# Second block's exponentials: rounded and full both from ScalarE, the low part from GpSimd

## The reference

```python
q = _conv1x1_bn(xf, q_w, ...)          # 16 channels
k = _conv1x1_bn(xf, k_w, ...)
v = _conv1x1_bn(xf, v_w, ...)          # 128 channels
attn = jax.nn.softmax(jnp.einsum('bci,bcj->bij', q, k), axis=-1)
out = jnp.einsum('bcj,bij->bci', v, attn).reshape(b_, c_, h_, w_)
return gamma[0] * out + x
```

## Time and profile before

| | us |
|---|---|
| median of 3 runs | 405.02 |
| lowest and highest of the 3 | 403.21 and 407.89 |
| span of the profiled execution | 403.1 |
| TensorE busy (matmuls) | 341.7 |
| VectorE busy | 260.5 |
| ScalarE busy | 198.8 |
| GpSimd busy | 27.3 |

### The profile page before, as it was taken

One profiled execution on the slowest core, in us unless ns is written; L12 is line 12 of the kernel. 1 busy time (PEld: TensorE's weight loads), 2 busy tenths in 40 slices (PEclk: granted clock), 3 DMA queues, 4 the chain that ended last, 5 costly groups with the idle time before them and its releaser, 6 DMA issues. The chain is left out here.

```text
span 403.1 us, 4422 instructions
## 1 busy us (share of the span) xinstructions
PE 341.7 (85%) x1408; PEld 237.8 (59%) x1408; DVE 260.5 (65%) x425; ACT 198.8 (49%) x351; POOL 27.3 (7%) x35
## 2 busy tenths in 40 slices
PE   3999777999998989999999899996599657597296
PEld 2853644785666847656775686672468356565162
DVE  1576777897598669876977797569397431301605
ACT  2445585646686646385685555667452433211000
POOL 3211100000021000002010000061001000100000
PEclk9999899999999699999998999996697957777579
DMA  7500000000000000000000000059600000000005
GB/s 247 188 0 2 0 1 0 2 0 0 2 0 3 0 0 2 0 0 2 0 0 0 0 0 0 0 192 411 230 2 0 0 2 0 0 0 2 1 0 208
DMA packets 5778, 15.08 MB, mean 37 GB/s; under 512 B 1294, under 2 KB 1998, under 8 KB 5762
## 3 DMA queue, kind: packets, MB, share of 16 engines
q0 software_dynamic: 2304, 8.39, 5.9%
q1 hardware_dynamic: 3458, 6.49, 4.6%
HBM read 12.78 MB, written 2.10 MB: 37 GB/s over the span
## 5 line engine op out<-in xcount | busy, mean ns | idle before, releaser
L373 PE MATMUL acc<-e,v0n 128*128 128x512 f32 x128 | 58.9, 595 | 0.9 <-DVE v0n L828 0.8
L659 ACT ACTIVATE e<-tile,nmax 128x1024 f32<-128x1024 f32 x22 | 24.5, 1115 | 38.8 <-DVE nmax L821 29.1
L860 DVE TENSOR_TENSOR e1l<-e,e1h 128x1024 fp32r<-128x1024 f32 x32 | 39.5, 1248 | 0.7
L373 PEld LDWEIGHTS acc<-e,v0n 128*128 128x128 f32 x128 | 23.5, 189 | 24.6 <-issue 20.1
L698 ACT ACTIVATE e<-tile 128x1024 f32<-128x1024 f32 x25 | 25.7, 1027 | 20.7 <-DVE e1l L860 13.9
L821 DVE TENSOR_REDUCE nmax<-tile 128x1 f32<-128x1024 f32 x22 | 26.9, 1222 | 11.0 <-PE tile L373 10.5
L864 DVE TENSOR_REDUCE nmax<-tile 128x1 f32<-128x1024 f32 x27 | 32.1, 1216 | 2.4 <-PE tile L373 2.4
L373 PE MATMUL tile<-ks,qs 96*128 96x512 f32 (+2 forms) x82 | 27.2, 426 | 6.1 <-ACT tile L688 4.2
L688 ACT ACTIVATE tile<-tile,nmax 128x1024 f32<-128x1024 f32 x27 | 29.4, 1087 | 3.0 <-DVE nmax L864 2.8
L857 DVE CAST e1h<-e 128x1024 fp32r<-128x1024 f32 x32 | 21.7, 687 | 3.5 <-ACT e L698 3.4
L373 PEld LDWEIGHTS tile<-ks,qs 96*128 96x128 f32 x82 | 15.3, 209 | 14.6 <-issue 8.1
(11 more groups left out here) (202 smaller groups left out, 678.6 us busy)
## 6 DMA issues: line engine op xcount, KB each, us to landing
cas_h<-in_cas_h_in POOLq DMA_DIRECT2D x8, 512.0 KB, 9.6
cas_l<-in_cas_l_in POOLq DMA_DIRECT2D x8, 512.0 KB, 10.4
xin<-in_x SPq DMA_DIRECT2D x4, 512.0 KB, 4.7
out<-xin SPq DMA_DIRECT2D x3, 512.0 KB, 2.6
zexp<-in_region_in SPq DMA_DIRECT2D x2, 360.0 KB, 4.7
out<-xin SPq DMA_DIRECT2D x2, 256.0 KB, 2.4
bins<-in_bins_in SPq DMA_DIRECT2D x1, 372.0 KB, 5.1
x3s<-in_near_in SPq DMA_DIRECT2D x1, 288.0 KB, 5.6
```

The source lines that it names most:

```text
L373: return nc.tensor.matmul(o, lhsT, rhs, start=start, stop=stop, skip_group_check=skip)
L659: nc.scalar.activation(e0[:, i % RING0, :], t[:, :], ACT.Exp, bias=nmax0[:, i:i + 1], accum_out=sum0[:, i:i + 1]).then_inc(s["e0_ready"], 1)
L860: vec.tensor_tensor(e1l[:, i % RING, :], e1[:, i % STAGE, :], e1h[:, i % RING, :].bitcast(F32), ALU.subtract).then_inc(s["e1l_ready"], 1)
```

## The change

The round `e1h` and the full `e1` are both written by ScalarE: it reads the score tile twice and takes the exponential twice, first with the short format as its output, then as float32. The wait on `e1_used` that stood ahead of VectorE's cast now stands ahead of ScalarE's first exponential. The subtraction moves from VectorE to GpSimd, which waits for `e1_ready` (and `e1_used`). The steps `e1h:*` leave the lists; TensorE's own order and all places in PSUM are as before.

```diff
@@ STEADY (the same is done in L12_ALL)
-    ... norm0:3 scoreT:0 scoreT:1 e1h:0 gram:4 scoreT:2 e1l:0 e1h:1 e1l:1 mix:2 scoreT:3 gram:5 e1h:2 attend:0 ...
+    ... norm0:3 scoreT:0 scoreT:1 gram:4 scoreT:2 e1l:0 e1l:1 mix:2 scoreT:3 gram:5 attend:0 ...
@@ ScalarE
                     elif name == "scoreT":
                         t = take(step)
 
+                        wait_past(act, s["e1_used"], b * CH + max(i - RING + 1, 0))
+                        nc.scalar.activation(e1h[:, i % RING, :], t[:, :], ACT.Exp).then_inc(s["e1h_ready"], 1)
                         wait_past(act, s["e1l_ready"], b * CH + max(i - STAGE + 1, 0))
                         nc.scalar.activation(e1[:, i % STAGE, :], t[:, :], ACT.Exp).then_inc(s["e1_ready"], 1)
@@ VectorE
-                    elif name == "e1h":
-                        dve.wait_ge(s["e1_ready"], b * CH + i + 1)
-
-                        wait_past(dve, s["e1_used"], b * CH + max(i - RING + 1, 0))
-                        vec.tensor_copy(e1h[:, i % RING, :], e1[:, i % STAGE, :]).then_inc(s["e1h_ready"], 1)
-                    elif name == "e1l":
-                        dve.wait_ge(s["e1h_ready"], b * CH + i + 1)
-                        vec.tensor_tensor(e1l[:, i % RING, :], e1[:, i % STAGE, :],
-                                          e1h[:, i % RING, :].bitcast(F32), ALU.subtract).then_inc(s["e1l_ready"], 1)
@@ GpSimd
+                    elif name == "e1l":
+                        pool.wait_ge(s["e1_ready"], b * CH + i + 1)
+                        wait_past(pool, s["e1_used"], b * CH + max(i - RING + 1, 0))
+                        gp.tensor_tensor(e1l[:, i % RING, :], e1[:, i % STAGE, :], e1h[:, i % RING, :].bitcast(F32),
+                                         ALU.subtract).then_inc(s["e1l_ready"], 1)
```

More of the change, by code:

```diff
@@ L79 @@
     "qkproj:0 qkproj:1 qklow:0 join elu:0 qklow:1 elu:1 zelu:0 zelu:1 score:0 score:1 score:2 score:3 "
[4 rows of a table removed]
-    "xkeep chanT")
[4 rows of a table added]
 END = steps(
```

## The result

The changed kernel takes 415.95 us (median of 4, 414.96 to 416.26), beside 405.51 for the kernel before (median of 4, 403.21 to 407.89): ratio 1.0248, 95% interval 1.0202 to 1.0295. It is slower by 10.4 us.

What follows compares the result with a forecast made beforehand. TensorE was taken as the bound, with no gap in the attend stretches of images 0 to 2. 9.0 there plus 2.2 in the last image, 11.2 us, on 405.0 gave 416; range 411 to 422.

Steps and rivals of the forecast that it cites:

- Part 1: VectorE losing its casts and subtractions: worth 0 in images 0 to 2, some 0.3 us at most in the last.
- Part 2: Second exponential on ScalarE in the attend stretches: its queue order delays TensorE by 2.3 to 2.4 us per image.
- Part 3: Subtraction on GpSimd at 2.40 us each: TensorE waits 0.6 us at the third product of `attend:7`, images 0 to 2.
- Images 0 to 2: Attend stretches of the first three images: 2.4 + 0.6 = 3.0 us each, 9.0 together (2.5 to 3.8 each).
- Part 4: Last image's attend stretch: `attend:0` 1.7 us late, `attend:4` ending 2.1 late by GpSimd; 2.2 taken, bounds 1.4 and 3.0.
- the low clock behind `xproj` follows as before: Last image, behind `attend:4`: `xproj` and its low clock unchanged, giving GpSimd time to finish by 314.2, needed at about 315.
- up to 0.7 was forecast: Last image: `x3:0` and `x3:1` on VectorE meet GpSimd's first subtraction, one waiting for the other, costing up to 0.7 us.
- the last one: Sum over the span: the last image's 2.2 us counted in full, added to the 9.0 for 11.2.
- Hidden: Rival: second exponential and subtraction hide in the attend stretches, so not slower, 404 to 406 us; chance 7%.
- chunk 3: Deciding point of the hidden rival: its rounded exponential must end by the start of `attend:1`, with `gram:5`'s right behind.
- A lower clock in the stretches of images 0 to 2: Rival: gaps around `scoreT:4` lower TensorE's clock once per image, 7.8 us more, 424; chance 10%.
- GpSimd at 2.8: Rival: GpSimd's subtraction takes 2.8 us and bounds the stretches, 4.5 to 4.7 per image, 4 in the last, 422; chance 8%.

Runs made afterwards that it cites:

- e1: The changed kernel with the subtraction back on VectorE, ScalarE still taking both exponentials: 413.5 us, ratio 1.023 to the kernel before.
- e5: The changed kernel with VectorE subtracting and four places for the rounded exponentials: 409.8 us, ratio 1.0105 to the kernel before.
- e4: The kernel before with a useless second exponential of each chunk on ScalarE, cast and subtraction left on VectorE: ratio 1.0099 by two executions (406.7 and 409.4 us).
- e3: The changed kernel with four places for the rounded exponentials instead of three: 410.5 us, ratio 1.0138 to the kernel before.
- e6: The kernel before with the change in the last image alone: 405.9 us, ratio 1.0005 to the kernel before.
- e7: The kernel before with the change in images 0 to 2 alone: 415.8 us, ratio 1.0235 to the kernel before.
- e2: The kernel before with only the subtraction moved to GpSimd, one exponential and VectorE's cast kept: 423.8 us by two executions; ratio 1.0552 takes in all four.
- e8: As e2, but VectorE rounds by a maximum over an axis of length one instead of a cast: 415.9 us, ratio 1.026 to the kernel before.

## Why the prediction was right

It said 416, by order in ScalarE's queue first and GpSimd second, and 415.95 was measured. The two causes are right and were shown in images 0 to 2. That the number agrees within a tenth is luck: the rise was forecast as 11.2 and is 10.4, on a kernel before whose median was taken as 405.0 and is 405.5 with one more run, and several misses below cancel. Point by point, by its own parts:

**Part 1, VectorE relieved: worth nothing.** Right. VectorE idles 12.7 us ahead of `gram:6`'s maximum now, and in images 0 to 2 there was no TensorE gap to close. In the last image the wait of 0.15 for VectorE's `e1l` is gone and one of 0.30 for ScalarE has come ahead of `scoreT:7`. VectorE lost 56 us of busy time, not 61, with 2 us of `x3:1` waiting for GpSimd in there; ScalarE gained 28, not 33, and GpSimd 76 as forecast.

**Part 2, the second exponential.** A rounded exponential takes 1.03 and starts 0.92 apart, as taken. 2.3 to 2.4 were forecast, e1 has 2.6. The gaps stand where they were put; by the starts above, `scoreT:2` lost 0.44 (forecast 0.3), `gram:5` 0.07 (0.2), `attend:0` 0.36 (0.35), `scoreT:4` 1.00 (0.75) and `scoreT:5` 0.62 (0.7). Of the two mechanisms in it, the second reading of a tile costs 1.0 to 1.2 (e5, e4), the wait for `attend` at the head of ScalarE's queue 1.4 to 1.6 (e1 less e4, e1 less e5), or 1.15 when GpSimd subtracts (the changed kernel less e3).

**Part 3, GpSimd.** The duration was taken as 2.40, and is 2.38 to 2.40 in the stretches of images 0 to 2. Forecast 0.6, measured 0.65 (the changed kernel's stretches less e1's), of which 0.43 stands at `attend:7`.

**Images 0 to 2.** 9.0 forecast, 9.8 measured: a term that was sized 0.27 per image too low, for the two pieces above.

**Part 4, the last image: right in sum by luck, largely wrong in how.** 2.2 forecast, 2.4 measured in the stretch. TensorE there, and a window of the clock:

```profile
302.88 0.70 PE L371 MATMUL tile<-qs,ks 96*128 96x512 f32 x2 [1.59 <-DVE v1l L850]
305.21 1.19 PE L371 MATMUL acc<-e1h,v1h 128*128 128x512 f32 x2 [1.63 <-ACT e L698]
...
303.80:307.80 4.00, 2.59 (x6) 2.14 (x7) 2.41 (x1) 3.10 (x4) 4.00 (x2) 0.50 0.00 0
...
310.46 0.64 PE L371 MATMUL acc<-e1h,v1l 128*128 128x512 f32 x2
...
317.54 3.75 PE L371 MATMUL acc<-winT,x3s 128*128 128x16 f32 x16
...
323.84 0.77 PE L371 MATMUL acc<-e1h,v1h 128*128 128x512 f32 x2
```

`attend:0` is 1.63 us late for ScalarE, as forecast (1.7). But "the low clock behind `xproj` follows as before" failed. The clock already fell in this wait (the window that is 0.50 throughout starts 1.4 ahead of `attend:0`): the granted clock was 0.50 from 305.2 to about 310.5, where the pairs of matmuls took 1.05, against 0.62 behind it. With that, `attend:4` ended 3.8 late (17.55 into the stretch, 13.78 before) and not the 2.1 that GpSimd's chain was to make it. The spell behind `xproj` then ended after 2.7 us (323.84), where before it lasted 5.3, and gave 1.4 back. Neither was in the prediction's sum. In e6, the same code in the last image, TensorE worked at the low clock for about 3.2 us there and not 5.2, and the stretch is 1.0 shorter, half of the difference: what this image costs depends on when the clock falls and returns. And GpSimd's chain was not the limit: it found gaps of 0.25 between its subtractions, and with VectorE subtracting the stretch was no shorter (e1, 28.20). VectorE's and GpSimd's rows show the two engines meeting where the prediction said:

```profile
301.50 1.23 DVE L850 TENSOR_TENSOR v1l<-tile,v1h 128x1024 fp32r<-128x1024 f32 x1 [3.32 <-ACT v1h L680]
302.65 3.56 DVE L912 SCALAR_TENSOR_TENSOR x3s<-zneg,sc,xkeep 128x512 f32<-128x512 f32 x2
...
303.32 7.45 POOL L1044 TENSOR_TENSOR e1l<-e,e1h 128x1024 fp32r<-128x1024 f32 x3 [20.18 <-ACT e L698]
```

`x3:0` and `x3:1` take 3.56 where two such took 1.5 alone: `x3:1` had to wait for GpSimd's first subtraction, 2.1 on VectorE where up to 0.7 was forecast. The longest of GpSimd's 32 subtractions took 2.82. Nobody waited for `x3:1`.

**A step that failed without harm to the number is the last one**, that what is lost in the last image stays lost. From images 0 to 2 nothing comes back (e7). Of the last image's 1.4 (e6) to 2.4, 1.46 came back in the `join` at full clock, so e6 measures nothing. The misses, +0.8 in images 0 to 2, +0.2 in the last stretch and -1.35 behind it, come to -0.3 on the 11.2: the span grew by 10.9.

**The rivals.** Hidden: no, and the point that it was to be decided at, chunk 3, decided it. A lower clock in the stretches of images 0 to 2: no, 1.00 in all three, with TensorE busy 22.49 of 24.45 in image 0. The clock fell where this rival did not look, in the last image. GpSimd at 2.8: no, 2.40 on average.

No version here beats the kernel before. Its stretch had TensorE at 21.11 of 21.20, so nothing that only relieves VectorE could.

Left open: why the `join` of the last image runs at full clock in most of these kernels. It takes 4.80 in all whose last stretch has a further wait of TensorE of 1.2 to 1.6 us in `attend:0`, be it for ScalarE (the changed kernel, e1, e3, e5, e6) or for GpSimd's `e1l` (e2, e8), and 6.26 to 6.28 in the two without it (the kernel before, e7). But e4's profiled execution has the wait, 1.28, and takes 6.27, so the wait alone does not decide it; it was not tried apart.

## What to carry to other kernels

Ask what the engine that sets the end waits for before moving work off a busy one: VectorE at 18.8 of 21.2 us looked crowded, but TensorE had no gap there to close, and 56 us less work for VectorE bought nothing. When a step moves to another in-order queue, its wait moves too, and everything queued behind it inherits that wait; here a ring of three places at the head of ScalarE's queue cost more than the slower engine did, and a fourth place won back a third of what the stretches had lost (4.1 of 12.2). Walking the queues with durations from the trace gave the stretches of images 0 to 2 within 0.5 us, except where two engines shared something that the walk didn't have (e2). In the last image, where the clock changes, the walks missed by up to 1.8 (e1). A total that comes out right doesn't show that each term is: compare stretch by stretch.

## What the runs showed of the hardware that was not expected

- VectorE's cast (SBUF to SBUF, float32 in) and GpSimd's subtraction exclude each other: a cast of 0.69 took 2.40 when it began behind a subtraction, and the pair set a pace of 3.01 per chunk (e2). VectorE's reduction over an axis of one does the rounding in 1.22 beside GpSimd, with no loss for either (e8), and the kernel went from 423.8 to 415.9.
- Most of the last image's delay cost nothing in the end: e6's stretch is 1.4 longer, and its time is that of the kernel before (ratio 1.0005), because a later piece ran 1.46 shorter at a granted clock of 1.00 in place of 0.76. Spans of the same code behind the last stretch ranged from 83.9 to 87.7 us over these kernels, and the first stretch began between 68.5 and 72.3, which is as much as some of the differences looked for. The lengths of the stretches of images 0 to 2 repeat within 0.1 us between kernels of the same code (changed and e7, before and e6) and told the variants apart where the times could not. The last image's does not: 27.81 and 26.82 for the same code.
